# Later normalisation, two pairs of banks and one column range per row in a four-layer graph kernel

## The reference

```python
# layer 0: masked attention
e = where(adj > 0, (x @ edge_w) @ (x @ edge_w).T, -9e15)
out = adj * (softmax(x @ node_w, axis=0) * softmax(e, axis=1)) @ (x @ weight) + bias
# layer 1: edge attention over adj, beside adj @ (x @ W_gcnb), both gated by adj @ x
# layer 2: relu(D (adj + I) D (x @ weight)), D = rowsum ** -0.5
# layer 3
h = relu(adj @ (x @ W1) + b1); h = relu(adj @ (h @ W2) + b2); out = adj @ (h @ W3) + b3
```

## Time and profile before

| | us |
|---|---|
| median of 3 runs | 790.58 (789.51 to 792.78) |
| the profiled execution | 791.85, of which 790.0 from the first to the last instruction (span) |
| TensorE matmuls busy | 744.8 (94%) in 4192 matmuls and as many weight loads |
| VectorE busy | 452.6 (57%) |
| ScalarE busy | 347.4 (44%) |
| GpSimd busy | 120.0 (15%) |
| mean granted TensorE clock | 0.988 of full |

### The profile page before, as it was taken

How to read it: one execution, slowest core, us unless ns; L and a number is a source line. 1 busy time by engine, 2 the same in 40 slices (tenths; PEclk the granted TensorE clock), 3 DMA queues, 4 the chain that set the end, 5 groups by cost and what they waited for, 6 DMA issues and landing times.

```text
span 790.0 us, 11567 instructions
## 1 busy us (share of the span) xinstructions
PE 744.8 (94%) x4192; PEld 489.8 (62%) x4192; DVE 452.6 (57%) x934; ACT 347.4 (44%) x530; POOL 120.0 (15%) x246
## 2 busy tenths in 40 slices
PE   7888999797999999999989999999999999999997
PEld 6776766564678878787835545675664546465343
DVE  4485888688768797988944475121271311114465
ACT  4678877675385474646722243132270322224000
POOL 2011222111321012111122340000001000000343
PEclk9998999998999999999999999999999999999999
DMA  8948889996568509400030000000000000000011
GB/s 230 180 91 146 162 164 159 167 155 112 103 95 153 88 2 159 68 2 1 1 87 1 0 0 1 1 0 0 0 0 27 1 1 0 0 0 0 21 41 46
DMA packets 114300, 48.71 MB, mean 62 GB/s; under 512 B 103504, under 2 KB 109776, under 8 KB 114256
## 3 DMA queue, kind: packets, MB, share of 16 engines
q1 hardware_dynamic: 110224, 33.44, 21.7%
q0 software_dynamic: 4032, 14.68, 11.2%
HBM read 35.53 MB, written 2.10 MB: 48 GB/s over the span
## 4 chain that ended last, share of the span: by engine, by line
PE 43%; DVE 7%; issue 3%; ACT 1%; POOL 1%; DVEq 0%; POOLq 0%; ACTq 0%
PE ps L777 11%; PE ps L928 11%; PE ps L904 8%; PE ps L963 4%; PE ps L937 3%; PE ps L887 3%; PE ps L953 2%; DVE stats L1297 1%; PE ps L633 1%; DVE es_lo L1285 1%; DVE x L1575 1%; DVE tm L1495 1%; DVE agg_lo L1483 1%; DVE y L1619 0%; DVE y L1697 0%
## 5 line engine op out<-in xcount | busy, mean ns | idle before, releaser
L777 PE MATMUL ps<-adjT,x 128*128 128x512 bf16 (+1 forms) x768 | 173.3, 379 | 5.1 <-DVE agg_lo L1483 2.5
L777 PEld LDWEIGHTS ps<-adjT,x 128*128 128x128 f16 x768 | 72.3, 98 | 90.4 <-issue 7.6
L696 PE MATMUL ps<-sup,turned 128*128 128x512 f16 x256 | 88.3, 393 | 12.1 <-DVE y L1350 12.1
L1285 DVE TENSOR_TENSOR hh_lo<-hf,hh_hi 128x512 fp32r<-128x512 f32 x32 | 22.2, 693 | 134.5 <-ACT hf L1221 133.5
L928 PE MATMUL ps<-adjT,G 128*128 x384 | 83.6, 379 | 0.4 <-ACT hf L1221 0.4
L819 PE MATMUL ps<-H_hi,es_hi 128*128 128x258 f32 x256 | 76.8, 300 | 2.2 <-DVE es_lo L1285 1.7
L819 PE MATMUL ps<-H_lo,es_hi 128*128 128x258 f32 x256 | 72.4, 283 | 0.0
L819 PE MATMUL ps<-H_hi,es_lo 128*128 128x258 f32 x256 | 72.4, 283 | 0.0
L698 PE MATMUL ps<-sup,turned 128*128 128x256 f16 x256 | 71.7, 280 | 0.0
L928 PEld LDWEIGHTS ps<-adjT,G 128*128 128x128 f16 x384 | 37.3, 98 | 45.4 <-issue 0.9
L492 POOL TENSOR_TENSOR rstd<-mv,epsc 128x1 f32<-128x1 f32 x64 | 15.2, 238 | 295.9 <-DVE mv L1299 295.9
(11 more groups left out here) (216 smaller groups left out, 1484.7 us busy)
## 6 DMA issues: line engine op xcount, KB each, us to landing
adjb<-in_adj POOLq DMA_DIRECT2D x16, 512.0 KB, 7.0
adjf<-in_adj POOLq DMA_DIRECT2D x12, 512.0 KB, 6.4
x<-in_x SPq DMA_DIRECT2D x4, 512.0 KB, 6.0
out<-adjf SPq DMA_DIRECT2D x16, 128.0 KB, 1.7
adjf<-in_L_gnn_W SPq DMA_DIRECT2D x1, 1024.0 KB, 5.9
W1f<-in_L_gnn_W SPq DMA_DIRECT2D x1, 512.0 KB, 3.7
adjf<-in_L_gnn_W SPq DMA_DIRECT2D x1, 512.0 KB, 3.9
we<-in_L_gnn_edge_w SPq DMA_DIRECT2D x1, 256.0 KB, 3.8
```

Source lines behind the costliest of these rows:

```text
L696: ins = mm(bank(6 + u), PT(HI, t)[:, jt, :], sup[:, jt, :], start=(jt == 0), stop=False, skip_group_check=True)
L777: ins = mm(bank(4 + f), x16[:, part, jt, f * P:(f + 1) * P], adj(b, jt), start=(jt == 0 and part == HI), stop=(jt == T - 1 and part == LO))
L1285: return tt(to, frm, high.bitcast(F32), ALU.subtract)
```

## The change

It has seven parts.

1. In `round0` VectorE applies the norm of an earlier tile right after the next maxima, and `final0` takes the tile that was summed in the same round, `SUMMED[t]`, as the round's last step.
2. `weighted` and `out3` use three (two) matmuls of 256 columns that all add into the same 256 columns; `final0` and `final3` read them with one instruction. The semaphore `xb_used` goes.
3. The load of adj row tile 4 (`LATER_LOADED`) is issued after tile 9's factor instead of tile 5's, and its DMA transpose stands behind the last `turn_p` instead of before the last tile's.
4. The start: the first two tiles of x come in a DMA of their own, `scores(0)` waits for each column block of h by itself, the mask of round 1 is built behind the support groups, ScalarE keeps rows 1, 2 and 3 before other work, and VectorE takes maxima(1) earlier; GpSimd adds the first two biases earlier and loads one tile fewer ahead of its reductions.
5. `aggregate` of layers 2 and 3 uses banks 4, 5 for even blocks and 6, 7 for odd ones, and waits for the reads of two blocks back.
6. The loops over b of layers 2 and 3's first half, and the last tiles' on VectorE, are written out, and wait for the diagonals of their own block alone; in layer 3 the last tile of `rows(B - 2)` comes behind the last `aggregate`.
7. `out3` uses banks 0 to 3 after the first four tiles.

```diff
@@ -105,7 +105,7 @@
-    LATER_LOADED = {5: 4}
+    LATER_LOADED = {9: 4}
...
+        def agg_bank(layer, b, f):
+            return 4 + f + (2 * (b % 2) if layer else 0)
...
+            sp.dma_start(x[:, 0:2, :], x_tiles[:, 0:2, :]).then_inc(x_first, 16)
             for c in range(B):
-                sp.dma_start(x[:, TB * c:TB * c + TB, :], x_tiles[:, TB * c:TB * c + TB, :]).then_inc(x_landed[c], 16)
+                tiles = slice(TB * c if c else 2, TB * c + TB)
+                sp.dma_start(x[:, tiles, :], x_tiles[:, tiles, :]).then_inc(x_landed[c], 16)
...
                 turn_p(t, LO)
-                if t == T - 2:
-                    sp.wait_ge(e_mm, B * T)
-                    turn_later(TB)
-
-            for t in (TB + 1,):
+            sp.wait_ge(e_mm, B * T)
+            for t in (TB, TB + 1):
                 turn_later(t)
...
-            for t in range(AB + 2):
+            for t in range(AB + 1):
                 load_adj(t)
+            bias_x(0, 0, pv_read)
+            bias_x(1, 1, pv_read)
             pool.wait_ge(node_max, 1)
...
@@ scores @@
-                if t == 0:
-                    pe.wait_ge(p0_lo, P0_SUP)
...
                 for c in range(B):
+                    if t == 0:
+                        pe.wait_ge(p0_lo, P0.index(("h", c, KD - 1)) + 1)
...
@@ weighted @@
-                    ins = mm(bank(6 + u), PT(HI, t)[:, jt, :], sup[:, jt, :], start=(jt == 0), stop=False,
-                             skip_group_check=True)
-                    ins = mm(bank(6 + u, D), PT(LO, t)[:, jt, :], sup[:, jt, 0:D], start=False, stop=(jt == T - 1),
-                             skip_group_check=True)
+                    for part, c0 in ((HI, 0), (HI, D), (LO, 0)):
+                        ins = mm(bank(6 + u, D), PT(part, t)[:, jt, :], sup[:, jt, c0:c0 + D],
+                                 start=(jt == 0 and (part, c0) == (HI, 0)), stop=(jt == T - 1 and part == LO))
...
@@ aggregate_tiles @@
-                        wait_from(pe, agg_lo, (layer * B + b) * KD + f - 1)
+                        n = layer * B + b
+                        if n == B + 1:
+                            pe.wait_ge(g_ev, B * TB)
+                        else:
+                            wait_from(pe, agg_lo, (n - 1 if n <= B else n - 2) * KD + f + 1)
...
-            pe.wait_ge(diag_added, T)
-            with pe.Fori(1, B) as b:
+            for b in range(1, B):
+                pe.wait_ge(diag_added, TB * (b + 1))
...
-            with pe.Fori(1, B) as b:
+            for b in range(1, B):
+                pe.wait_ge(diag_gone, TB * (b + 1))
                 aggregate(2, b, 0)
                 hidden1(b - 1)
-                rows(b - 1, W2s, HID)
+                rows(b - 1, W2s, HID, tiles=range(TB - (b == B - 1)))
                 aggregate(2, b, 1)
+            rows(B - 2, W2s, HID, tiles=(TB - 1,))
...
@@ out3 @@
-                t, u = TB * b + k, k % 2
-                if not (isinstance(b, int) and k < 2):
-                    pe.wait_ge(o3_read, t - 1)
+                if not isinstance(b, int):
+                    pe.wait_ge(o3_read, TB * b + k - TB + 1)
                 for jt in range(T):
-                    ins = mm(bank(u), adjT[...], f16[:, jt, :], start=(jt == 0), stop=(jt == T - 1))
+                    for part in (HI, LO):
+                        ins = mm(bank(k, D), adjT[...], f16[:, jt, part * D:part * D + D], start=(jt == 0 and part == HI),
+                                 stop=(jt == T - 1 and part == LO))
...
@@ ScalarE @@
-            for n in range(P0_SUP + 2, P0_SUP + 6):
+            for n in range(P0_SUP + 2, P0_SUP + 7):
                 group0(n)
             p_high(0)
+            for n in range(P0_SUP + 7, P0_GROUPS):
+                group0(n)
             make_fill(1)
-            for n in range(P0_SUP + 6, P0_GROUPS):
-                group0(n)
             place_row0()
+            keep_row(1)
             act.wait_ge(node_neg, 1)
...
-            keep_row(1)
...
             make_fill(2)
+            keep_row(2)
             exp_row(1)
-            keep_row(2)
...
-                if t > 2:
+                if t > TB - 1:
                     keep_row(t)
                 if t + 1 < T:
                     make_fill(t + 1)
+                if t + 1 == TB - 1:
+                    keep_row(t + 1)
                 exp_row(t)
...
@@ VectorE @@
-                stt(y[:, u, :], bank(6 + u, D), rowf[:, u, 2:3], xb[:, u, :], ALU.mult, ALU.add).then_inc(xb_used, 1)
-                dve.wait_ge(xb_used, t + 1)
-                stt(y[:, u, :], ps[:, 6 + u, D:2 * D], rowf[:, u, 2:3], y[:, u, :], ALU.mult, ALU.add) \
-                    .then_inc(pv_read, 1)
+                stt(y[:, u, :], bank(6 + u, D), rowf[:, u, 2:3], xb[:, u, :], ALU.mult, ALU.add).then_inc(pv_read, 1)
...
-                maxima(t, u)
-                p_low(t - 1, 1 - u)
-                m = SUMMED.get(t - 1)
-                if m is not None:
-                    final0(m, m % 2)
+                maxima(t, t % 2)
+                if t - 1 in SUMMED:
+                    m = SUMMED[t - 1]
+                    normed(m, m % 2, x[:, m, :])
+                p_low(t - 1, (t - 1) % 2)
                 conv_first(LOW_ROUND.get(t, ()))
-                if m is not None:
-                    normed(m, m % 2, x[:, m, :])
+                if t in SUMMED:
+                    final0(SUMMED[t], SUMMED[t] % 2)
...
             p_low(0, 0)
+            maxima(1, 1)
             dve.wait_ge(node_gmax, 1)
...
-                stt(y[:, u, :], bank(at, D), g1[:, 3:4], xb[:, u, :], ALU.mult, ALU.add).then_inc(xb_used, 1)
-                dve.wait_ge(xb_used, T + t + 1)
-                stt(y[:, u, :], ps[:, at, D:2 * D], g1[:, 3:4], y[:, u, :], ALU.mult, ALU.add).then_inc(o3_read, 1)
+                stt(y[:, u, :], bank(at, D), g1[:, 3:4], xb[:, u, :], ALU.mult, ALU.add).then_inc(o3_read, 1)
```

More of the change, by code:

```diff
@@ L776, in aggregate_tiles @@
                     for part in (HI, LO):
-                        ins = mm(bank(4 + f), x16[:, part, jt, f * P:(f + 1) * P],
+                        ins = mm(bank(agg_bank(layer, b, f)), x16[:, part, jt, f * P:(f + 1) * P],
                                  adj(b, jt), start=(jt == 0 and part == HI),
@@ L889, in hidden1, with rows @@
                     ins.then_inc(h_mm, 1)
-            def rows(b, ws, width, last=False, uncounted=0):
-                for k in range(TB):
+            def rows(b, ws, width, last=False, uncounted=0, tiles=range(TB)):
+                for k in tiles:
                     n = b * TB + k
@@ L952, in _ @@
                 for k in range(TB):
-                    ins = mm(bank(4 + k), adjT[:, 0, jt, k * P:(k + 1) * P], f16[:, jt, :], start=(i == 0),
-                             stop=(i == T - 1))
+                    for part in (HI, LO):
+                        ins = mm(bank(4 + k, D), adjT[:, 0, jt, k * P:(k + 1) * P], f16[:, jt, part * D:part * D + D],
+                                 start=(i == 0 and part == HI), stop=(i == T - 1 and part == LO))
                     if i == T - 1:
@@ L1098, in agg_high @@
                 act.wait_ge(agg_mm, (layer * B + b) * KD + f + 1)
-                run(agg[HI][:, f, :], bank(4 + f), ACT.Copy, scale=1.0 / XS).then_inc(agg_hi, 1)
+                run(agg[HI][:, f, :], bank(agg_bank(layer, b, f)), ACT.Copy, scale=1.0 / XS).then_inc(agg_hi, 1)
             def edge_exp(b, pair):
@@ L1193, in _ @@
             agg_high(1, 0, 0)
-            with act.Fori(1, B) as b:
+            for b in range(1, B):
                 agg_high(1, b - 1, 1)
@@ L1221, in hidden, with rows @@
                 run(hf[:, o % 2, :], bank(frm), ACT.Relu, bias=bias[:, o:o + 1], scale=scale).then_inc(h_f, 1)
-            def rows(b, to, first, width):
-                for k in range(TB):
+            def rows(b, to, first, width, tiles=range(TB)):
+                for k in tiles:
                     act.wait_ge(r_mm, b * TB + k + 1)
@@ L1230, in mid @@
                     hidden(b, o, o % 2, b1c, 1.0)
-                rows(b, G, AHEAD, HID)
+                rows(b, G, AHEAD, HID, range(TB - (b == B - 2)))
             agg_high(2, 0, 0)
-            with act.Fori(1, B) as b:
+            for b in range(1, B):
                 agg_high(2, b - 1, 1)
@@ L1238, in _ @@
             agg_high(2, B - 1, 1)
+            rows(B - 2, G, AHEAD, HID, (TB - 1,))
             for o in range(KH):
@@ L1429, in _ @@
             scale_of(1)
-            maxima(1, 1)
             for c in range(TB):
@@ L1445, in _ @@
                     weight_parts()
+            conv_first(range(9, 12))
             p_low(T - 1, 1)
-            conv_first(range(9, 11))
-            final0(T - 4, 0)
-            conv_first(range(11, 12))
             normed(T - 4, 0, x[:, T - 4, :])
@@ L1626, in _ @@
             agg_low(1, 0, 0)
-            with dve.Fori(1, B) as b:
-                own.enter(b - 1, TB)
+            for b in range(1, B):
                 agg_low(1, b - 1, 1)
@@ L1631, in _ @@
```

(7 more changed lines are left out.)

34 lines of the change are left out of this document (16 added, 18 removed).

## The result

The kernel after takes 773.94 us (median of 4 runs, 773.62 to 774.99) where the kernel before took 791.68 in the same measurement (789.51 to 792.83): a ratio of 0.977, 95% interval 0.9745 to 0.9796. 17.7 us are gained, 25.3 were forecast. The profiled execution takes 773.62 us, its span is 771.8 us. Single executions of some of them lie over 20 us apart; there the lowest and the highest time are given as well.

A forecast was written before the change was run, and what follows sets the result against it. Layer 0's TensorE waits and the resulting slow clock were taken as the bound. 14.2 + 4.5 - 1.0 + 6.2 + 2.1 + 0.5 - 1.2 = 25.3 us gave 765 us, own range 760 to 769 (chance 0.50), wide range 757 to 776.

The forecast's parts named there:

- rivals 1 and 2: Layer 0: transposes set the rounds, 770 us, chance 0.20; a collision or slow clock stays, 771 to 775 us, chance 0.14.
- The signs that were named: Whole trace: weighted(15) ends near 196 us, two reads gone, norms 0.40 us, no mid-round low transpose over 4 us.
- the rounds' 14.2 us: Layer 0's rounds: TensorE sets them; of 17.6 us stalls and slow clock all but 3.4 go, gain 14.2 us.
- Rival 1: Layer 0's late rounds: high transposes' landings make rounds 8.5 us, costing 4 to 5 us; time 770, chance 0.20.
- The late load's 6.4 us: Adj row 4's load in layer 0: its collision with a low transpose costs 6.4 us, inside the 17.6 us.
- The start: Before layer 0's round 5: scores(5) at 80.0 instead of 84.5 us, gain 4.5 us, bounds 0 and 6.
- The clock: TensorE's pauses before rounds 4 and 5: slow clock at the second could lose up to 2.9 us; 1 us set.
- signs of being wrong: 256-column matmuls 0.15 us or more apart, TensorE waits over 1 us in more than three rounds, repeated low clock in layer 0.
- Later layers and out3: Behind layer 0: paired banks and own diagonals gain 6.2 us, out3's four banks 2.1, final3's dropped read 0.5.
- 256 columns: weighted and out3: narrower matmuls cost 0.6 us each, the 512 added weight loads run under the matmul before.
- rival 4: 256-column matmuls: added weight loads not hidden, 0.10 us each, 51 us; time 816 us, slower, chance 0.03.
- Rule and row of VectorE's norm: VectorE's norm in layer 0: 0.82 us is waiting for GpSimd's xb; 0.40 us in its new place, 0.41 us gained.

The follow-up runs named there:

- e3: Kernel after with VectorE's round in the old order (low part, step on the tile summed a round earlier, norm last): 792.57 us (774.89 to 797.00).
- e6: Kernel before with one edit, row 4's late load issued with round 9 and its transpose behind the last one of layer 0: 787.74 us, ratio 0.9953.
- e11: Kernel after with layer 0's row products as before: one matmul of 512 columns and one of 256, and VectorE's second read: 779.65 us.
- e7: Kernel after with layer 0's loads of adjacency rows 8 to 15 cut to 128 of 2048 columns (other output): 769.02 us, ratio 0.9726.
- e4: Kernel after with adj row 4's load again behind tile 5's factor, its transpose ahead of the last tile's: 776.23 us (773.99 to 778.42).
- e12: Kernel after with layer 0's loads waiting for ScalarE's fill, kept copies before high parts from row 10, second bias behind reductions, row 7 later: 771.29 us, ratio 0.9746.
- e1: Kernel after with GpSimd's first two biases behind its three reductions instead of ahead of them: 793.89 us (781.76 to 795.55).
- e8: Kernel after with both first biases behind the reductions and loads of rows 8 to 15 cut to 128 columns: 776.43 us (772.04 to 779.04).
- e10: Kernel after with loads from row 8 waiting for a high transpose's landing, second bias between loads 5 and 6, row 7 one iteration later: 791.24 us (786.64 to 797.63).
- e5: Kernel before with only the parts for layers 1 to 3 (paired banks, own diagonals, moved rows tile, four out3 banks): 784.43 us, ratio 0.9906.

## Why the prediction was right, and where its sum was wrong

- *Direction and mechanism*: right. The read at L1350 is gone, the moved norm takes 0.40 to 0.41 us in the rounds without a wait, VectorE's read of a sum no longer holds TensorE. That this comes with the order, and not with the late load, the start or the single read, is what e3, e6 and e11 show together. How much of the time it is worth isn't told apart: of the 10.4 us of the rounds, the late load alone gives 2.7 in e6's traced rounds (3.3 to 3.7 us of its time), and the rest has no experiment of its own, since e3's and e11's traces have jams.
- *The number*: 773.94 us lies within 757 to 776, but outside the forecast's own 760 to 769. The wide range holds it because it takes in rivals 1 and 2 (770 and 771 to 775), and parts of both came: landings that hold up the rounds, and a slow clock behind one early pause.
- *The signs that were named*: `weighted(15)` ends at 202.75 instead of near 196 us. The others came: the two reads are gone, the norms take 0.40 us, no low transpose of the middle rounds lasts over 3.2 us, no `agg_lo` wait is left, the matmuls are 0.109 us apart, TensorE waits over 1 us twice behind `weighted(5)` (1.2 and 2.2 us), and the clock is low in one stretch of layer 0. So the number of 765 us fell short, and none of the signs of being wrong came.
- *The term that was mis-sized most beside the start is the rounds' 14.2 us* (with its claim that TensorE sets them): 10.4 us measured. Rival 1 named the reason and bounded it at 4 to 5 us, and e7 gives 4.5 us back when the loads shrink. The argument against it was that late rounds have no loads beside them. In the kernel after the mask's loads are issued up to 145.16 us (round 11), and the moved late load itself at 163.63 us, in round 13, 1.4 us behind a high transpose that lands after 6.5 us. Most of what e7 gives back, 3.2 of 4.5 us, comes behind the start of `weighted(11)` (164.84 against 166.63), where its smaller loads are already over: earlier delays seem to use up a lead that the last rounds then lack. That is a reading of the two traces, not a test.
- *The late load's 6.4 us* inside that term: too much. e6 got 3.3 to 3.7 us by moving it alone, and in the new order e4's traced rounds show nothing of it. Its wait was one of eight; with the load moved, e6 has nine that make the same sum; a wait's length in a list is not its price.
- *The start*: 4.5 - 1.0 us forecast, none left at `weighted(5)`. This is the largest miss: 3.5 of the 7.1 us. The walk of the lists was right up to `scores(4)` (67.51 measured and 71.99 before: 4.5 us), and `scores(5)` came at 82.81 where 80.0 was forecast. Between them stand the low transpose's 10.4 us landing and GpSimd's pause. e12 removes both at once and starts `weighted(5)` 4.2 us earlier; which of the two cost more isn't told apart, since e1, e8 and e10, which moved the pause, met other jams. The same start code varies by 2 us: 116.50, 115.86 and 114.17 in before, e6 and e5.
- *The clock*: 1 us was set for pauses of the start. `scores(4)`, behind a wait of 2.0 us, ran at full clock; behind one of 2.4 us 4.2 us of `scores(5)` ran at a granted 0.59, mostly the lower of the two levels. From its start to the next sum it takes 5.97 us (88.78 - 82.81) against 4.39 before, which is 1.6 us lost. So of the start's 4.5 us 1.7 were there at `scores(5)`, and the clock took 1.6 of them. In the late rounds the clock was not low.
- *Later layers and out3*: 6.2 + 2.1 + 0.5 - 0.6 = 8.2 us forecast, 7.8 measured, and e5 shows the same 7.8 without the new layer 0. The wait before `out2(3)` stayed, as said.
- *256 columns*: right. The chain that ended last in the kernel after:

```profile
724.65 41.93 PE ps L975 x384
```

  41.93 / 384 = 0.109 us each, 0.218 for the two that replace the 0.216 us of the earlier trace rows; in layer 0 a tile's 48 take 5.24 us. So all 512 added weight loads stayed under the matmuls, and rival 4 is out. The rule of the Trainium skill, TensorE: Matmul & The Clock Gate, Part 3, that a weight load overlaps running matmuls only when their row groups differ, is contradicted once more as it stands. The same section also lets a load run ahead into a background weight buffer; no run here shows whether that is what happens.
- *Rule and row of VectorE's norm*: 0.82 us at 76.59, where GpSimd's `xb` runs from 76.53, and 0.41 us at 139.08 with GpSimd idle. By the Trainium skill, SBUF — State Buffer, Who interferes with whom, VectorE in a two-port mode and GpSimd exclude each other at the port pair that they share; the trace agrees (0.82 against 0.41 us).

Of the 7.1 us by which the execution fell short (25.3 forecast, 18.2 found), 3.5 are the start with its clock, 0.4 the later layers with out3, and 3.2 the rounds (13.6 after the columns' 0.6, 10.4 measured).

## What to carry to other kernels

When the chain that sets a loop is shortened, ask which chain comes next and price it with the neighbours it will have; here it was the landing of DMA transposes, which the loads beside them stretch. A wait in the list is worth its length only if nothing behind it would have waited too: take it away alone and look before adding it to a sum. And where GpSimd goes from reductions to elementwise work, let the first such instruction be one that nobody waits for.

## What the runs showed of the hardware

- A load of 512 KB from GpSimd's queue and a transpose of 512 KB from SyncE's, issued close together, can slow each other far beyond what they take alone (loads of 6 to 7 us landed after 17.1 us in e3 and 23.2 in e10). With neither a load nor another transpose near it, a transpose of the row products mostly lands after 4.3 to 4.4 us (the exceptions took up to 6.2). With a full load 0.28 to 0.34 us behind a high one it landed after 12.7, 14.8 and 20.3 us (three of three); 0.5 to 0.6 us behind, after 8.1 to 8.8 and once 24.0; at 1.3 to 2 us behind, high ones landed after 6.1 to 8, and once, in e12, after 4.5. With a load of 32 KB 0.30 and 0.31 us behind (once each in e7 and e8), it landed after 4.6 and 4.7 us. The distance doesn't decide alone: in e12 three high ones with loads 2.8 to 3.8 us behind took 10.2 to 10.9 us, and in e1 and e8 two with loads on both sides took 17.0 and 14.0. While the jam of e1 lasts, the DMA share is 1.28 and 77 GB/s move instead of 166. Why is open: only issue times and landings are seen.
- GpSimd pauses 6.8 to 10.3 us in front of its first elementwise instruction behind `partition_all_reduce`, with no instruction in the profile: 9.84 us before, 10.06 after, 6.77 in e1, 8.74 in e12, 10.29 in e4. The Trainium skill, GPSIMD Engine Reference, 2.1 Instruction dispatch, says that the first call to a freshly loaded kernel pays some 6 us of code loading without a visible instruction. The rows agree in kind (a pause without an instruction) and are longer; no run here shows that it is code loading.
